# Two attention stages, six experts and a feed-forward on one core: stage borders reordered, queries, maxima and moments of a block issued earlier

## The reference

```python
x = x + _L0_xattn_ref(_layernorm(x), ctx, mask, Wq, bq, Wk, bk, Wv, bv, Wo, bo)   # 16 heads of 16, mask added
x = x + _L0_ffn_ref(_layernorm(x), proj_w, anchors, routing_temp, w1, w2)         # 6 experts 256->128->256, top 2 by a router
x = x + _L1_xattn_ref(_layernorm(x), ctx, ctx, w_q, w_kv, w_concat)               # 16 query heads, one key/value head
x = x + _L1_ffn_ref(_layernorm(x), w1, b1, w2, b2)                                # 256->1024->256, piecewise linear gelu, fixed point
```

## Time and profile before

| what | us |
|---|---|
| median of 3 runs | 892.53 |
| the three runs | 890.9 to 894.1 |
| the profiled execution, its own time | 892.31 |
| its span in the profile | 890.5 |

### The profile page before, as it was taken

The page is one execution under the profiler, slowest core; times in us unless marked ns, Lnnn a source line. Parts: engine busy times, 40 slices in busy tenths (PEclk is TensorE's granted clock), DMA queues, the critical chain, the costliest instruction groups (busy, mean ns, idle before and its releaser), DMA issues.

```text
span 890.5 us, 13722 instructions
## 1 busy us (share of the span) xinstructions
PE 783.8 (88%) x4452; PEld 577.4 (65%) x4452; DVE 660.3 (74%) x1576; ACT 520.1 (58%) x942; POOL 397.4 (45%) x323
## 2 busy tenths in 40 slices
PE   4789999999886999999978988888878989999996
PEld 2556566666555787877854455444457878888885
DVE  6468777777756777877776888888757788977774
ACT  4245655555452446554435666566658777788774
POOL 3623322213213344344310222222138999899995
PEclk9989999999998999999968999999989999999999
DMA  8855533455200000001055555654000000000001
GB/s 291 124 108 107 136 63 74 86 105 99 68 0 1 1 1 6 2 1 49 1 73 73 73 72 73 120 72 68 8 1 1 1 24 25 25 24 1 24 24 49
DMA packets 24817, 48.01 MB, mean 54 GB/s; under 512 B 3655, under 2 KB 6856, under 8 KB 24234
## 3 DMA queue, kind: packets, MB, share of 16 engines
q1 hardware_dynamic: 22792, 42.87, 26.1%
q10 hardware_dynamic: 1954, 4.26, 1.3%
HBM read 11.47 MB, written 4.19 MB: 18 GB/s over the span
## 4 chain that ended last, share of the span: by engine, by line
PE 53%; DVE 17%; POOL 8%; issue 7%; ACT 6%; DMA 6%; ACTq 1%; SPq 0%; DVEq 0%; POOLq 0%
PE bank L135 16%; PE bank L371 5%; PE bank L396 5%; PE bank L777 5%; PE bank L629 5%; PE bank L421 5%; PE bank L407 4%; DMA qst<-mt 4%; POOL eex L508 3%; DVE mx L327 3%; PE bank L399 2%; POOL fy L696 2%; DVE x L597 2%; PE bank L121 2%; DMA qst<-ml 2%
## 5 line engine op out<-in xcount | busy, mean ns | idle before, releaser
L301 ACT ACTIVATE pt<-bank 77x512 f32<-77x512 f32 x256 | 146.3, 589 | 125.8 <-PE bank L399 76.9
L327 DVE TENSOR_REDUCE mx<-bank 128x4 f32<-128x308 f32 x256 | 110.0, 472 | 38.3 <-PE bank L374 24.9
L396 PE MATMUL bank<-qst,l_kst 128*77 128x512 f32 (+1 forms) x256 | 106.6, 431 | 20.8 <-DMA qst<-mt 13.3
L696 POOL TENSOR_TENSOR fy<-fpart,fg 128x512 f32<-128x512 f32 x64 | 103.1, 1611 | 9.3 <-DVE fpart L737 4.7
L371 PE MATMUL bank<-l_kblk,qh 128*128 128x308 f32 x256 | 91.5, 372 | 14.7 <-DVE mx L327 13.5
L103 POOL TENSOR_TENSOR rstd<-var,minus_half 128x4 f32<-128x4 f32 x32 | 32.7, 1023 | 139.4 <-DVE var L98 90.2
L689 POOL TENSOR_TENSOR frise<-fg,fg 128x512 f32<-128x512 f32 x64 | 90.6, 1415 | 9.0 <-POOL fy L696 4.6
L396 PEld LDWEIGHTS bank<-qst,l_kst 128*77 128x77 f32 (+1 forms) x256 | 36.8, 149 | 85.0 <-issue 49.8
L371 PEld LDWEIGHTS bank<-l_kblk,qh 128*128 128x128 f32 x256 | 50.6, 198 | 58.0 <-issue 50.8
L277 POOL TENSOR_TENSOR ol<-ot,oh 128x512 fp32r<-128x512 f32 x32 | 43.1, 1345 | 97.8 <-ACT oh L306 63.3
L597 DVE SCALAR_TENSOR_TENSOR x<-bank,eweight,x 128x256 f32<-128x256 f32 x192 | 79.6, 476 | 5.4 <-PE bank L629 5.1
(11 more groups left out here) (179 smaller groups left out, 2162.0 us busy)
## 6 DMA issues: line engine op xcount, KB each, us to landing
qst<-qh SPq DMA_DIRECT2D x64, 256.0 KB, 6.4
qst<-ql SPq DMA_DIRECT2D x32, 256.0 KB, 9.3
out<-x SPq DMA_DIRECT2D x8, 512.0 KB, 2.6
qst<-ml SPq DMA_DIRECT2D x8, 480.0 KB
x<-in_x ACTq DMA_DIRECT2D x3, 1024.0 KB, 11.0
weights<-in_mlp_w SPq DMA_DIRECT2D x2, 1024.0 KB, 5.1
mraw<-in_mask SPq DMA_DIRECT2D x8, 154.0 KB
x<-in_x SPq DMA_DIRECT2D x2, 512.0 KB, 5.8
```

Of the source, the lines that this page charges most:

```text
L301: self.nc.scalar.activation(self.pt[0:T, i // 4 % 2, i % 4, :], self.bank_of(G, i)[0:T, :], ACT.Exp).then_inc(self.probs, 1)
L327: self.nc.vector.reduce_max(out, banks[u % len(banks)][:, 0:4 * T].rearrange("q (p par t) -> q p par t", p=2, par=2), AX.X).then_inc(self. ...
L396: last = self.nc.tensor.matmul(out, layer.kst[rows, layer.stack(c * HC + 2 * k + par), b * T:(b + 1) * T], self.qst[rows, self.slot(G), c ...
L696: self.nc.gpsimd.tensor_tensor(self.y[:, k % 2, :], self.part[:, k % 2, :], self.g0[:, k % self.R, :], ALU.add).then_inc(self.y_ready, 1)
```

## The change

**Inside both attentions.** On PE, the queries of a block stand after scores 14 and 15 of the block two before it, instead of after scores 0 and 1 of the block before it. The 16 units of maxima are spread over scores 0 to 9 by a table, and `turn_maxima` stands after score 11. On ACT the `leading` of a block's queries follows the last exp of the block two before, and the copy of `mt` stands one exp earlier. On DVE the order in a block is now: reductions 0 to 2, divide of p, reduction 3, fold of p, 4 to 8, divide 0, 9 to 13, first add, 14 and 15, second add, divide 1, fold, two `norm.rest` of nm, divide 2, the two `rest` of the queries of nm, and the moments of nm+1. In block 0 the units stand four scores later.

```diff
+UNITS = ((0,), (1, 2), (3,), (4, 5), (6, 7), (8,), (9, 10), (11, 12), (13,), (14, 15))
...
 # PE, second attention
                         att.score(pe, l1, G, i)
-                        if i < C and n < 2 * BLOCKS:
-                            att.queries(pe, l1, n, i)
                         if i == 1 and p >= BLOCKS:
                             att.weigh(pe, l1, p, 3)
-                        if 3 <= i <= 10 and n < 2 * BLOCKS:
-                            for u in (2 * (i - 3), 2 * (i - 3) + 1):
+                        if i < len(UNITS) and n < 2 * BLOCKS:
+                            for u in UNITS[i]:
                                 att.max_unit(pe, l1, n, u, att.X)
...
+                        if i in (14, 15) and nm < LN_FFN:
+                            att.queries(pe, l1, n + 1, i - 14)
...
 # DVE, second attention, end of a block
                     att.divide(dve, G, 2)
+                    if n == 2 * BLOCKS:
+                        ff.early(dve, 1)
+                    if nm < LN_FFN:
+                        for c in range(C):
+                            att.rest(dve, n + 1, c)
+                    if nm <= LN_FFN:
...
+                        norm.moments(dve, nm + 1)
```

```diff
+                pe.wait_ge(kblk_ready, 1)
+                pe.wait_ge(id5_ready, 1)
+                for u in range(16):
+                    att.max_unit(pe, l0, 0, u, FIRST_MAX)
+                att.turn_maxima(pe, 0, FIRST_MAX[0])
                 pe.wait_ge(vo_in, 64)
...
-                pe.wait_ge(kst_in, 16 * 12)
+                pe.wait_ge(kst_in[0], 16 * 6)
                 pe.wait_ge(kst_const, 2)
                 pe.wait_ge(v_ready, 2)
 
+                for c in range(C):
+                    att.queries(pe, l0, 1, c)
```

```diff
                 att.weigh(pe, l0, BLOCKS - 1, 3)
-                ex.hidden(pe, 0, 2)
                 pe.wait_ge(ex.router_ready, 1)
                 pe.wait_ge(att.unfolded, 4 * BLOCKS)
                 ex.project(pe, 0)
+                ex.hidden(pe, 0, 2)
+                pe.wait_ge(att.probs, H * BLOCKS)
+                ex.compare(pe, 0)
                 ex.hidden(pe, 0, 3)
```

More of the change, by code:

```diff
@@ L1083, in _ @@
                                          ACT.Copy).then_inc(kst_const, 1)
-                nc.scalar.activation(att.id5[:], id5f[:], ACT.Copy).then_inc(id5_ready, 1)
-                norm.norm(act, 0)
-                for c in range(C):
-                    norm.lead(act, 0, c, att.W[c], att.xh)
-                for c in range(C):
-                    att.leading(act, 0, c)
+                att.maxima(act, 0, FIRST_MAX[0])
+                norm.norm(act, 1)
                 act.wait_ge(v_clear, 2)
@@ L1183, in _ @@
                             norm.lead(act, nm, h - 12, att.W[h - 12], att.xh if nm < LN_FFN else ff.xh[0])
+                        if h == H - 1 and nm < LN_FFN:
+                            for c in range(C):
+                                att.leading(act, n + 1, c)
                         if G in (BLOCKS + 1, BLOCKS + 2) and h in (7, 14):
@@ L1297, in _ @@
                     att.divide(dve, G, 2)
+                    if nm < BLOCKS:
+                        for c in range(C):
+                            att.rest(dve, nm, c)
+                    if nm <= BLOCKS:
+                        if G == 1:
+                            dve.wait_ge(xr_in, 16 * 2)
+                        if nm + 1 >= BLOCKS:
+                            dve.wait_ge(att.added, 2 * (nm + 2 - BLOCKS))
+                        norm.moments(dve, nm + 1)
                 att.divide(dve, BLOCKS - 1, 3)
@@ L1301, in _ @@
                 dve.wait_ge(ex.cleared, 2)
-                for e in range(2):
-                    ex.rest(dve, 0, e)
+                ex.rest(dve, 0, 0)
+                ex.router(dve, 0)
+                ex.rest(dve, 0, 1)
                 for k in range(2):
@@ L1327, in _ @@
                             norm.moments(dve, nm + 1)
-                for c in range(C):
-                    att.rest(dve, BLOCKS, c)
-                ex.add(dve, BLOCKS - 1, 4)
-                att.take_maxima(dve, BLOCKS, range(0, 8), FIRST_MAX1)
-                ex.add(dve, BLOCKS - 1, 5)
-                att.take_maxima(dve, BLOCKS, range(8, 16), FIRST_MAX1)
+                att.rest(dve, BLOCKS, 0)
+                att.take_maxima(dve, BLOCKS, range(0, 4), FIRST_MAX1)
+                att.rest(dve, BLOCKS, 1)
@@ L1334, in _ @@
+                att.take_maxima(dve, BLOCKS, range(4, 16), FIRST_MAX1)
+                for e in (4, 5):
+                    ex.add(dve, BLOCKS - 1, e)
                 for c in range(C):
                     norm.rest(dve, LN_ATT1 + 1, c, att.W[c], att.xh, att.xl)
+                dve.wait_ge(ex.added, ALL_EXP)
+                norm.moments(dve, LN_ATT1 + 2)
+                for c in range(C):
+                    att.rest(dve, BLOCKS + 1, c)
                 for G in range(BLOCKS, 2 * BLOCKS):
@@ L1338, in _ @@
                     p, n, nm = G - 1, G + 1, LN_ATT1 + G - BLOCKS + 2
[L1339 to L1343 removed]
                     if n < 2 * BLOCKS:
[L1345 to L1347 removed]
+                        att.take_maxima(dve, n, range(0, 3), att.X)
@@ L1544, in _ @@
                 pe.wait_ge(kst1_const, 2)
+                for c in range(C):
+                    att.queries(pe, l1, BLOCKS + 1, c)
                 for G in range(BLOCKS, 2 * BLOCKS):
```

157 lines of the change are left out of this document (83 added, 74 removed).

## The result

The changed kernel takes 906.19 us (median of 4 runs, 905.29 to 907.1), the kernel before 893.32 in the same comparison: a ratio of 1.0161, with a 95% interval of 1.014 to 1.0181. It is slower by 12.9 us. The profiled execution has a span of 903.7 us where before had 890.5, so 13.2 us are to be found in it.

A forecast was written before the change was run, and what follows sets the result against it. PE was taken as near its limit in the first attention, a chain of waits as setting the second. Borders -18.3 and blocks +27.6 us gave +9.3 on 892.31: 901.6, said as 902; range 877 to 915, the forecast's own 894 to 912.

The forecast's parts named there:

- The walk through a block: Both attentions: new order laid over old distances; DVE's order makes PE wait, +2.5 us a block in first, +2.1 in second.
- The second attention: Blocks 9 to 14: each takes 26.2 us and not 24.1, +12.6 us for six blocks.
- I keep 1.00 in the sum: Second attention's blocks: granted clock stays 1.00 despite four PE waits of 1 to 2 us each, so no clock cost added.
- rival 3: Both attentions: lower PE clock costs each of 12 blocks 0.5 to 1.5 us more, +6 to +18, about 914; chance 0.10.
- Experts' start: Start of the experts: POOL's power starts 5.3 to 5.9 us earlier, at about 263.6; -5.5 us, bounds -4.5 and -6.5.
- Block 7: First attention's block 7: no units there, and DVE has the same work ahead of the divide; 0 us.
- Start of the program: Up to block 0's weigh 2: earlier mask DMA and queries bring score 0 at about 43.5; -7.3 us, bounds -4.5 and -9.
- second attention's start: Block 8: turn_maxima starts at 455.9 instead of 461.53, partly offset by moved work; -2.5 us, bounds 0 and -4.5.
- feed-forward's start: Feed-forward: conversions done by 651.8, so hidden 2's 3.0 us wait goes; -3.0 us, bounds -2 and -3.5.
- Rival 1: Both attentions: waits at units 5 to 8 and 11 halve; +1.5 and +0.4 us a block, 885.4; chance 0.20.
- Rival 2: Both attentions: moments cost nothing, blocks gain about 1 us each, giving 862; chance 0.09.
- Rival 4: Borders between stages: moved waits are replaced by others, half of the 18.3 us stays, 911; chance 0.06.

The follow-up runs named there:

- the filled block 14: Changed kernel with unit 1's matmul issued 14 times and unit 4's 10 times in blocks 9 to 14 of the second attention: 898.6 us (one run).
- the kernel that beats both: Changed borders, first attention with early queries and units at scores 3 to 10, second attention with the blocks of before: 871.05 us, ratio 0.9774 to the kernel before.
- the borders alone: Changed kernel with the loops of the kernel before from block 1 (first attention) and block 9 (second) on: 877.7 us, ratio 0.9848 to the kernel before.
- the run with both edits: Changed kernel with units back at scores 3 to 10, DVE's order of before, and moments ahead of the two ql: 871.26 us, ratio 0.9766.
- the units late: Changed kernel with units back at scores 3 to 10, turn_maxima at 12, DVE's reductions, divides, fold and adds ordered as before: 882.4 us (one run).
- the moments first: Changed kernel with the moments of the norm ahead of the two ql in both attentions: 890.02 us, ratio 0.998 to the kernel before.

## Why the prediction was right, and where its sizes were not

The forecast (slower, 902.0 us, 894 to 912 for its own case) is the case that came: 906.2.

- **The walk through a block** was right in its mechanism. In the first attention it gives 28.8 us, and 28.56 came. Unit 2 waits 1.35 (said 1.65), unit 5 0.93 (1.05), unit 11 0.43 (0.6), the queries 0.34 (0.6). Each is ended by the releaser that was named. The moments ahead of `ql` take away unit 2's wait and nothing else; with reduction 3 moved, the wait of unit 5 moves on.
- **The second attention** is the term that was mis-sized: +12.6 predicted, +22.1 measured. The waits ahead of the queries and of units 2 and 5 are nearly those of the walk (0.86, 1.93 and 1.38 against 1.0, 2.0 and 1.7); unit 11 waits 0.49 against 1.2, and 1.15 in the filled block 14, at 1.00. The step that failed is "I keep 1.00 in the sum", with its reason that the idle of 1.34 us in the earlier trace rows did not take the clock down. The granted clock is 0.82 to 0.88. With the waits filled and the clock at 1.00, three blocks take 26.0 us against 27.8 without the filling, so the clock is 1.8 us of each.
- **The walk itself was a little short there.** These three filled blocks lie 2.2 us over the same three of before, where the walk says 2.1; but two of those three ran at 0.93. Over the same three of the kernel that beats both, which has the blocks of before at 1.00 (22.75, 23.37, 23.23), they lie 2.9. What the other 0.8 us are I did not find.
- **The clock was rival 3**, at 0.5 to 1.5 us in each of 12 blocks and a chance of 0.10. It came in six of them. They lie 9.5 us over the walk, 1.6 each; the filling gave back 5.8, and that the rest is the clock too is not shown. The price in rows 1, 24.54 against 24.08, was read from two different blocks; the same block at 0.93 and 1.00 took 24.51 and 23.28. The Trainium skill, TensorE: Matmul & The Clock Gate, "HAM oscillation — how this bites in real kernels", tells of short groups of matmuls that run at half rate again and again, each behind a wait for a DMA; the waits of its case are longer than any in these blocks, a condition that the prediction left out when it drew "0.93 or worse" from it. Here the clock fell with the shorter waits of the second attention too, and with those of the first, 1.35 and 0.93 us, it stayed at 1.00.
- **Experts' start**: -5.5 predicted, -9.8 measured. The power came 7.2 us sooner against "5.3 to 5.9". Before, `hidden` 2 waited 1.94 us for `ehh` and ran at the lower clock, and the projection stood behind it; now the projection is issued first, at the full clock. What each of the two is worth no run separates; in the eight kernels with the new borders the power starts 11.9 to 12.0 us behind the weigh 2 of block 7, where before it was 19.1. The other 2.6 us are behind the power, and 2.0 of them are the clock by the run with 30 matmuls. There the step that failed is the same one: a long idle costs also what follows it.
- **Block 7**: 0 predicted, -3.6 measured: the `mt` wait, a shorter wait for POOL's `ol`, and the clock behind it. The prediction put this term at nothing, looking at DVE's order alone and not at PE's waits.
- **Start of the program** -6.2 (said -7.3, within its bounds), **second attention's start** -1.5 (-2.5), **feed-forward's start** -3.1 (-3.0). In the first, the wait for `mh` at 1.28 us was foreseen at 1.6.
- **Borders and blocks as a sum.** By the spans the borders alone give 14.9 us, where the prediction has 18.3, and the blocks' part is 28.1, where it has 27.6. Both agree better than single terms do: block 1 pays 4.5 us in the run with the borders alone, and the blocks' part holds the -3.6 of block 7 beside the +9.5 of the second attention. In the table +9.5 stands against -4.3 (experts), -3.6 (block 7) and -1.0 (first attention). That the total lies within 4 us of the forecast is luck in this part; a total that fits does not prove its terms.
- **Rival 1** (the later waits shrink) did not come, since divide 3 and divide 0 stand where they stand; the run with reduction 3 moved shows that moving this one reduction does not help. Only unit 11's wait in the second attention was mostly shorter, and there PE came late, at the low clock. **Rival 2** (the blocks gain) is what the run with both edits gives: 26.00 and 23.95 us, but only with another order of DVE, which the change does not have. **Rival 4** did not come: the borders alone gave 14.9 of the 18.3 us.

What stays open: why the second attention's clock falls with one long idle of 1.28 us (0.93 with the units late) or 1.38 us (0.81 with the moments first), while the kernel before, with 1.34 us, held 1.00 in blocks 9, 10, 11 and 13 and had 0.93 in 12 and 14, in 14 not in every execution; and why three of the filled blocks stay at 0.94. The place of the idle in the block differs, and so does what PE does between two of them; no run here tells these apart.

## What to carry to other kernels

An engine that works in order must have its long piece of unrelated work (here 2.0 us of moments, which cost up to 1.5 us a block) ahead of the instruction that others wait for, while its operand is still being made, and not behind it. When a consumer chain with two buffers is moved right behind its producer, everything that stood as cover between them must be counted: the same reductions that were hidden behind four scores and a weigh cost 2.5 us a block without them (1.1 to 3.2, depending on the moments and the stage). And where a walk through a block ends with TensorE idle more than once, give the clock a term of its own: filling the waits gave back 5.8 of the 22.1 us that the second attention had lost. Its price is to be read from one and the same block at both levels.

## What the runs showed of the hardware

- Idle TensorE time can be paid twice. Behind 1.93 and 1.38 us of idle in the second attention, matmuls of 308 columns took 0.60 us and not 0.38, and a weigh 1.93 and not 1.06, for some ten microseconds. Twenty-two useless matmuls a block made three blocks 1.3 to 2.7 us shorter; thirty of them in an idle of 6.74 us made the kernel before 2.0 us faster between two powers.
- In the first attention, where PE is busy 25.5 of 28.6 us, idle of 1.35 and 0.93 us left the clock at 1.00; in the second, busy for 21.0 us before, idle of 1.93 and 1.38 us went with 0.82 to 0.88.
- The same block of the second attention took 24.51 us at a granted clock of 0.93 and 23.28 at 1.00, in two executions.
- Two `ol` subtractions on POOL took 3.23 us where they began 0.5 us ahead of DVE's cast of 128x1536, and the cast then took 1.58. Where they began together with the cast, within 0.1 us, they took 4.7 to 4.8 us and the cast 0.92.
